# Scores for the softmax maxima in 32x32 tiles of TensorE: four matmuls of 32 queries in place of one of 128

## The reference

```
q = layernorm(x) @ Wq + bq;  k = ctx @ Wk + bk;  v = ctx @ Wv + bv      (per head: 128 x 16)
energy = q k^T, masked where mask == 0 (one mask for all batches)
attn   = softmax(energy / 4) over the keys;   out = (attn v) @ Wo + bo
x = x + tanh(g_xattn) * out
x = x + tanh(g_ffn) * tanh(((layernorm(x) @ W) @ A1) @ A2 + bias)
```

## Time and profile before

| | |
|---|---|
| median of three runs | 1079.83 us |
| the profiled execution, its own time | 1079.94 us |
| its span, first to last instruction | 1078.1 us |
| mean granted TensorE clock | 0.992 |
| TensorE matmuls busy | 95% of the span |
| VectorE busy | 88% |
| ScalarE, GpSimd busy | 77%, 75% |
| DMA, mean over the span | 147 GB/s |

### The profile page before, as it was taken

One profiled execution on the slowest core, in us unless ns is written; L12 is line 12 of the kernel. 1 busy time (PEld: TensorE's weight loads), 2 busy tenths in 40 slices (PEclk: granted clock), 3 DMA queues, 4 the chain that ended last, 5 costly groups with the idle time before them and its releaser, 6 DMA issues.

```text
span 1078.1 us, 45335 instructions
## 1 busy us (share of the span) xinstructions
PE 1023.4 (95%) x18487; PEld 892.2 (83%) x18487; DVE 948.6 (88%) x1331; ACT 828.6 (77%) x1275; POOL 806.0 (75%) x1184
## 2 busy tenths in 40 slices
PE   5988999999999999999999999999999999999965
PEld 5777888888888888888888888888888888888855
DVE  5778999998899999989999998899998999999866
ACT  4566888888788888878888788788887887878742
POOL 5245878878788887878888877788787887888753
PEclk9999999999999999999999999999999999999998
DMA  5133555555555555555555556555555555555431
GB/s 154 45 104 106 165 147 161 162 155 152 155 153 164 145 171 155 164 149 149 165 154 162 157 145 173 143 161 159 152 164 150 150 163 149 167 152 154 124 124 69
DMA packets 260400, 158.87 MB, mean 147 GB/s; under 512 B 174945, under 2 KB 227170, under 8 KB 260194
## 3 DMA queue, kind: packets, MB, share of 16 engines
q1 hardware_dynamic: 260050, 155.72, 51.4%
q10 hardware_dynamic: 144, 0.26, 0.1%
HBM read 85.92 MB, written 68.94 MB: 144 GB/s over the span
## 4 chain that ended last, share of the span: by engine, by line
PE 55%; DMA 13%; SPq 13%; issue 7%; POOL 6%; DVE 5%; ACT 1%; POOLq 0%; DVEq 0%; ACTq 0%
PE ps_m L507 11%; PE ps_m L500 11%; PE ps_s L636 9%; PE ps_s L615 8%; PE ps_x L647 7%; PE ps_m L574 5%; DMA scratch_y<-yn 5%; SPq L215 3%; DMA scratch_m<-max_T 3%; PE ps_s L621 3%; SPq L303 2%; SPq L292 2%; DMA q_aug<-scratch_m 2%; PE ps_m L494 2%; DMA den_wide<-scratch_r 2%
## 5 line engine op out<-in xcount | busy, mean ns | idle before, releaser
L1021 DVE TENSOR_TENSOR probs<-ps_s,far_T 128x2048 f32<-128x2048 f32 x128 | 293.3, 2291 | 60.0 <-PE ps_s L636 59.8
L1010 DVE TENSOR_REDUCE neg_max<-ps_s 128x16 f32<-128x2048 f32 x128 | 292.5, 2285 | 26.7 <-PE ps_s L621 26.2
L810 ACT ACTIVATE probs<-probs 128x2048 f32<-128x2048 f32 x128 | 245.0, 1914 | 6.2 <-DVE probs L1021 5.9
L785 ACT ACTIVATE q_aug<-ps_m,q_bias,q_scale 128x256 f32<-128x256 f32 x256 | 123.5, 563 | 58.0 <-PE ps_m L500 48.9
L615 PE MATMUL ps_s<-k_aug,q_aug 32*128 32x128 f32 x4096 | 150.6, 283 | 14.2 <-DVE probs L1021 8.1
L636 PE MATMUL ps_s<-q_aug,k_aug 32*128 32x128 f32 x4096 | 152.1, 283 | 8.5 <-DMA q_aug<-scratch_m 5.8
L615 PEld LDWEIGHTS ps_s<-k_aug,q_aug 32*128 32x128 f32 x4096 | 127.9, 186 | 34.9 <-issue 24.3
L636 PEld LDWEIGHTS ps_s<-q_aug,k_aug 32*128 32x128 f32 x4096 | 127.7, 186 | 27.3 <-DMA q_aug<-scratch_m 9.4
L647 PE MATMUL ps_x<-probs,v_ones 128*32 128x128 f32 x4096 | 139.2, 277 | 3.2 <-issue 2.4
L785 ACT ACTIVATE k_aug<-ps_m,k_bias,parity 128x256 f32<-128x256 f32 x256 | 123.5, 563 | 18.8 <-PE ps_m L500 18.8
L647 PEld LDWEIGHTS ps_x<-probs,v_ones 128*32 128x32 f32 x4096 | 104.7, 110 | 32.7 <-issue 32.6
(11 more groups left out here) (123 smaller groups left out, 1725.9 us busy)
## 6 DMA issues: line engine op xcount, KB each, us to landing
scratch_a<-a_den SPq DMA_DIRECT2D x64, 512.0 KB, 3.7
x_in<-in_x SPq DMA_DIRECT2D x64, 256.0 KB, 4.4
a_rows<-scratch_a SPq DMA_DIRECT2D x64, 256.0 KB
den_wide<-scratch_r SPq DMA_DIRECT2D x64, 256.0 KB
out<-y SPq DMA_DIRECT2D x64, 256.0 KB, 4.7
ctx_in<-in_ctx SPq DMA_DIRECT2D x252, 64.0 KB, 2.7
scratch_y<-yn SPq DMA_DIRECT2D x59, 256.0 KB, 4.3
y_blocks<-scratch_y SPq DMA_DIRECT2D x236, 64.0 KB, 2.4
```

What stands on the lines that cost most here:

```text
L785: last = nc.scalar.activation(dst[:, :, 2 * m + a, :], src[:, m * TOK:(m + 1) * TOK].rearrange("p (n q) -> p n q", q=P), ACT.Identity, bia ...
L810: nc.scalar.activation(tile, tile, ACT.Exp).then_inc(probs_ready, 1)
L1010: nc.vector.tensor_reduce(neg_max[:, 0:H].rearrange("p (j c) -> p j c", j=G), ps_s[:], AX.X, ALU.max, negate=True).then_inc(max_ready, 1)
L1021: nc.vector.tensor_tensor(probs[i % 2][:].rearrange("p j s q -> p (j s) q"), ps_s[:].rearrange("p j s q -> p (j s) q"), far_T[:].unsqueeze ...
```

## The change

In `scores`, the matmul of 128 queries at tile position (j * 32, 0) becomes four matmuls of 32 queries at (j * 32, c * 32), each writing its 32 partitions of the same bank. The keys, the flags and the order over `s` and `j` stay, and so does all else: the mask matmuls, the turned scores, the waits.

```diff
@@ -612,8 +612,10 @@
                 for s in range(SLOTS):
                     for j in range(G):
                         rows = slice(j * ROWS, (j + 1) * ROWS)
-                        nc.tensor.matmul(ps_s[:, j, s, :], q_aug[p % 2][rows, n, s, :], k_aug[p % 2][rows, n, s, :],
-                                         start=(s == 0), stop=False, tile_position=(j * ROWS, 0), skip_group_check=True)
+                        for c in range(G):
+                            part = slice(c * ROWS, (c + 1) * ROWS)
+                            nc.tensor.matmul(ps_s[part, j, s, :], q_aug[p % 2][rows, n, s, part], k_aug[p % 2][rows, n, s, :],
+                                             start=(s == 0), stop=False, tile_position=(j * ROWS, c * ROWS), skip_group_check=True)
```

## The result

The changed kernel takes 1422.43 us (median of four runs, 1408.56 to 1446.64) against 1081.59 us for the kernel before on the same chip: 1.309 times, interval 1.2945 to 1.3235. I had forecast 1070 us with a range up to 1165. 341 us were lost (difference of the medians).

What follows compares the result with a forecast made beforehand. The prediction took the `ps_s` loop, closed by TensorE and VectorE nearly tied, as the bound. From 1079.9 us it took 64 odd batches x 0.15 = 9.6 us, with feed and fetch at 0: 1070 us, range 1062 to 1165.

Steps and rivals of the forecast that it cites:

- What bounds the kernel: Loop over `ps_s`: TensorE and VectorE nearly tied, so a shorter score stage counts only in odd batches.
- the half in which VectorE is late: Even batches: the filler before the maxima ends after the mask starts, so shorter scores gain 0 there.
- Array time and what gets shorter: Scores and mask: sixteen tiles run side by side, first score to last mask start 1.15 to 1.00 us a batch.
- The drain: Between scores and mask: 0.20 us for draining the array and changing tiles was to fall away.
- a call is two pairs ..., so 6.6 ns a tile: Scores: filling sixteen tiles at 3.3 ns a load and matmul pair takes 0.10 us for the last tile.
- rival 1: First score to last mask: queue fed too slowly, costing from 8.0 ns a pair; 1154 to 1227 us; chance 0.25.
- The two bounds, 3.3 and 16: Queue feed in scores and mask: ns a pair, costing nothing at the lower, 147 us at the upper; below 7 taken.
- Instruction fetch: TensorE's instruction queue q8: 2.41 MB grows to 4.0 MB, 1.7% of the DMA engines, costed at 0.
- the feed rival: Same as rival 1: TensorE's queue fed too slowly between first score and last mask; chance 0.25.
- Rival 2: Score stage: the 0.15 us gain a batch doesn't reach the end, time stays 1078 to 1082 us; chance 0.19.
- Rival 3: Scores: four fp32 tiles of one row group share the way in, +32 us to +345 us; chance 0.07.
- Rival 4: Scores and mask: matmul start floor, 25 ns a pair +314 us, 29 ns +390 us (1470 us); chance 0.05.

Runs made afterwards that it cites:

- the small pairs: Kernel before plus 96 one-column bf16 matmuls a batch between scores and mask, scores unchanged: 1448.62 us, 1.339 times the kernel before.
- the stream: Kernel before plus 2048 one-column pairs in 32x32 tiles behind TensorE's last work, almost nothing else running: 1136.57 us, 1.0502 times the kernel before.
- the spread run: Kernel before plus 192 one-column matmuls per pair of batches, in groups of eight behind projection matmuls: 2118.6 us.

## Why the prediction was wrong

**What bounds the kernel: right.** The loop over `ps_s` and the half in which VectorE is late hold: with scores 0.76 us shorter the mean period of a batch (batches 10 to 119) fell only from 7.93 to 7.84 us.

**Array time and what gets shorter: wrong in the sum.** The drain did go away, and eight tiles side by side cost next to nothing in the array (32x64 tiles: 1.14 us); for sixteen tiles of fp32 that is not shown. But the step "a call is two pairs ..., so 6.6 ns a tile" took the 3.3 ns of the earlier trace rows for a lasting rate. It held for the first sixteen tiles and no longer: only the first 32 pairs of a stage go as fast, presumably those that the queue already held. A long stream goes at 7.7 to 8.3 ns a pair in four runs. Scores and mask were to end their starts after 1.00 us; it was 1.80 against 1.15 before. This is my rival 1 in kind, "144 pairs x rate - 1.15 us" with 12.5 ns a pair in effect: 0.65 us, +83 us by its formula against about 95 by the fit. I knew no row over 32 pairs and still took the lower end. The two bounds, 3.3 and 16, stood; the choice between them by "the nearest row" was the error, since the nearest in form was the farthest in length.

**Instruction fetch: the failed step.** "I cost it at 0, with the upper end inside the feed rival." I compared bytes (1.0% of the DMA engines) where the limit is a time for each page: 3.79 us, two pages in store. The trace of before had a sign of it. 147 packets in 1078 us are one in 7.3 us, and no two were nearer than 3.60 us: a little over half of the possible rate was in use. 243 packets x 3.79 us = 921 us, 0.85 of the old span: this alone should have made the step a rival with a price, since a burst of 352 instructions in 2 us takes 1.4 pages where half a page arrives. Standstills and the clock that falls after them were some 260 us of the loss by the fit. The step is shown by the small pairs that give the same standstills with the old scores, by the stream, and by the packets of q8 that end some 1.4 us before the end of each standstill.

The Trainium skill, "Runtime: NRT & Kernel Launch", section "Instruction fetch mechanics", says that instructions are refilled in blocks of 256, which the packages of 128 pairs agree with, and that the fetch stays hidden since the sequencer needs about 20 cycles for an instruction. The trace does not agree with that: the stream ran at some 4 ns an instruction and stood still after each block.

**The clock: not in the prediction.** After the standstill above, the matmuls ran at 1.2 GHz (L500 2.79 us instead of 1.70), and 41 of the 46 stretches at 1.2 GHz in the changed kernel begin in a standstill or soon after one. Mean granted clock 0.922 after 0.992; the fit puts some 75 us on it.

**The rivals.** Rival 2 (no gain) is out. Rival 3 (row groups) can't be the main cause, since the standstills come with the old scores too, but for the 95 us of slower scores it is open: its sign, steps of one tile longer than 0.11 us, is there (434 ns for a tile's two matmuls). Rival 4, the floor of 25 ns a pair, came near the measured time (1393 by the page's figure, 1470 by rows) for a wrong reason: "TensorE: Matmul & The Clock Gate" of the Trainium skill, section "Wait — 56ns, not 53.3ns?", has that floor, and the traces agree with it for pairs in one tile (25 ns apart in the spread run) but not for pairs spread over sixteen tiles, where streams of 96 and 128 pairs show 8 ns. A rival's number that fits is no proof of it.

**Range and chances.** Slower had 0.37, and nothing in the range reached 1422, because rival 1 counted only what scores and mask lose within a batch and took the feed as one rate. It is two: the queue's and the pages'.

## What to carry to other kernels

Count TensorE's instructions, not only its time: an fp32 call is four of them, and in a stream here 256 instructions came once in 3.79 us on average, so a stretch whose instructions go at under 15 ns each lives on what is in store; here bursts of 352 instructions a batch gave 90 standstills and bursts of 224 still 25 to 41, and after long ones the clock fell. Before cutting a matmul into tiles, compare the packets of the instruction queue and their least distance with the new count, stage by stage. Where precision is not needed, a narrower type takes away instructions and array time at once; here smaller tiles with the streamed side as long as before only added instructions.

## What the runs showed of the hardware

- A page of TensorE's instructions (256) takes 3.79 us in a steady stream with the core otherwise idle; 530 instructions ran before its first standstill. The page's packet ends 1.3 to 1.5 us before its instructions start.
- A long stream of pairs over sixteen 32x32 tiles starts one in 7.7 to 8.3 ns, at 1.2 as at 2.4 GHz; sixteen mask pairs went 3.3 ns apart. One-column pairs in one tile start 25 ns apart.
- A group of eight one-column matmuls in a two-column form between 128x128 matmuls costs 0.44 us at a granted clock of 1.00, 0.2 of it at 25 ns a matmul: 2118.6 us for a kernel with no standstill at all.
- With the tile form shared, there was no gap between fp32 and bf16 matmuls: the mask began among the last scores, where it had been 0.20 us behind the last one.
